# An attention-style block with three-pass fp32 matmuls: inputs centred before their split, and running maxima turned on VectorE

## The reference

```python
xn  = (x - mean_g) / sqrt(var_g + 1e-5)      # group norm, 32 groups of 8 channels, over all 4096 positions
q, k, v = split(xn @ W_qkv)                  # each 4096 x 256
k   = softmax(k over the 4096 positions)     # per channel
ctx = k^T v                                  # 256 x 256
out = x + (q ctx) @ W_out + b_out
```

## Time and profile before

| | |
|---|---|
| median of 3 runs | 1215.09 us (1214.95 to 1216.85) |
| the profiled execution | 1214.93 us, its span 1213.2 us |
| PE busy | 1190.1 us, 98% |
| DVE busy | 842.1 us, 69% |
| ACT busy | 840.1 us, 69% |
| POOL busy | 622.4 us, 51% |
| chain that ended last | PE 93%, DVE 2%, ACT 1%, POOL 1% |

### The profile page before, as it was taken

One profiled execution on the slowest core, in us unless ns is written; L12 is line 12 of the kernel. 1 busy time (PEld: TensorE's weight loads), 2 busy tenths in 40 slices (PEclk: granted clock), 3 DMA queues, 4 the chain that ended last, 5 costly groups with the idle time before them and its releaser, 6 DMA issues.

```text
span 1213.2 us, 21447 instructions
## 1 busy us (share of the span) xinstructions
PE 1190.1 (98%) x8460; PEld 1115.8 (92%) x8460; DVE 842.1 (69%) x1582; ACT 840.1 (69%) x1140; POOL 622.4 (51%) x288
## 2 busy tenths in 40 slices
PE   4999999999999999999999999999999999999998
PEld 4998999999899998999989999899999989999897
DVE  6877667676776767768776677766767676676551
ACT  5767768677685776757677686776857768577664
POOL 8664564635645355563655636356463564536520
PEclk9999999999999999999999999999999999999999
DMA  9448666576765758666486665867657576573524
GB/s 339 146 167 294 218 235 205 195 269 208 274 203 199 264 172 294 226 206 237 162 301 229 221 227 183 286 209 252 204 201 263 193 278 225 201 252 122 191 74 170
DMA packets 107077, 266.71 MB, mean 220 GB/s; under 512 B 10208, under 2 KB 10208, under 8 KB 106976
## 3 DMA queue, kind: packets, MB, share of 16 engines
q1 hardware_dynamic: 106976, 265.33, 63.5%
HBM read 198.18 MB, written 67.11 MB: 219 GB/s over the span
## 4 chain that ended last, share of the span: by engine, by line
PE 93%; DVE 2%; ACT 1%; POOL 1%; DMA 1%; issue 1%; SPq 0%; DVEq 0%; POOLq 0%; ACTq 0%
PE ps_k L399 29%; PE ps_e L564 19%; PE ps_e L573 10%; PE ps_g L492 5%; PE ps_e L480 5%; PE ps_e L492 5%; PE ps_e L482 5%; PE ps_g L480 4%; PE ps_g L482 4%; PE ps_g L511 1%; PE ps_g L528 1%; PE ps_g L542 1%; PE ps_g L534 1%; POOL x_lo L347 1%; DVE mx L892 1%
## 5 line engine op out<-in xcount | busy, mean ns | idle before, releaser
L341 POOL TENSOR_TENSOR xt_lo<-xt_raw,xt_hi 128x1024 fp32r<-128x1024 f32 x128 | 307.4, 2404 | 434.5 <-ACT xt_hi L676 309.1
L347 POOL TENSOR_TENSOR x_lo<-x_raw,x_hi 128x1024 fp32r<-128x1024 f32 x128 | 281.4, 2216 | 65.6 <-ACT x_hi L681 56.2
L892 DVE TENSOR_TENSOR mx<-ps_k,mx 128x256 f32<-128x256 f32 x480 | 203.3, 424 | 95.8 <-ACT e_raw L685 74.3
L733 ACT ACTIVATE o_stage<-ps_e,bias 128x512 f32<-128x512 f32 x253 | 170.9, 689 | 114.1 <-PE ps_e L573 114.1
L399 PE MATMUL ps_k<-wk_hi,xt_hi 128*128 128x256 f32 x1024 | 207.1, 284 | 1.0 <-DVE mx L892 0.7
L399 PE MATMUL ps_k<-wk_lo,xt_hi 128*128 128x256 f32 x1024 | 205.5, 283 | 0.0
L685 ACT ACTIVATE e_raw<-ps_k 128x512 f32<-128x512 f32 x256 | 141.4, 596 | 87.2 <-PE ps_k L399 87.2
L849 DVE BATCH_NORM_STATS2 bn<-xs 128x6 f32<-128x512 f32 x240 | 154.5, 686 | 40.7 <-DMA xs<-in_xt_dram 39.5
L693 ACT ACTIVATE e_hi<-e_raw 128x1024 fp32r<-128x1024 f32 x128 | 135.1, 1055 | 60.9 <-DVE e_raw L917 33.0
L399 PEld LDWEIGHTS ps_k<-wk_hi,xt_hi 128*128 128x128 f32 x1024 | 163.4, 190 | 8.7 <-issue 1.8
L399 PE MATMUL ps_k<-wk_hi,xt_lo 128*128 128x256 f32 x1024 | 158.2, 283 | 0.0
(11 more groups left out here) (129 smaller groups left out, 1992.7 us busy)
## 6 DMA issues: line engine op xcount, KB each, us to landing
xt_raw<-in_xt_dram SPq DMA_DIRECT2D x128, 512.0 KB, 4.3
x_raw<-in_xn_dram SPq DMA_DIRECT2D x128, 512.0 KB, 3.5
out_dram<-o_stage SPq DMA_DIRECT2D x127, 512.0 KB, 4.5
xs<-in_xt_dram SPq DMA_DIRECT2D x240, 256.0 KB, 5.1
w_setup<-in_w_dram SPq DMA_DIRECT2D x2, 256.0 KB, 10.1
out_dram<-o_stage SPq DMA_DIRECT2D x2, 256.0 KB, 2.0
wk<-in_w_dram SPq DMA_DIRECT2D x1, 256.0 KB, 9.9
wq_t<-in_w_dram SPq DMA_DIRECT2D x1, 256.0 KB, 10.9
```

The source lines that it names most:

```text
L341: nc.gpsimd.tensor_tensor(xt_lo[:, s], xt_raw[:, s], xt_hi[:, s].bitcast(F32), ALU.subtract).then_inc(xt_lo_ready, 1)
L347: nc.gpsimd.tensor_tensor(x_lo[:, s], x_raw[:, s], x_hi[:, s, :, 0:C].bitcast(F32), ALU.subtract).then_inc(x_lo_ready, 1)
L733: nc.scalar.activation(o_stage[:, u % O_SLOTS, h, :], src, ACT.Identity, bias=bias[:, h:h + 1]).then_inc(o_ready, 1)
L892: nc.vector.tensor_tensor(mx[:], tile, mx[:], ALU.max).then_inc(max_done, 1)
```

## The change

1. For images behind the first, ScalarE takes the high part of `xt` plus minus the mean (two instructions of 128 x 512 for one of 128 x 1024), and GpSimd adds minus the mean to `xt_raw` in place (`xt_centre`, two instructions of 128 x 512) before `xt_low`. The output then needs no product of the matrix with the mean: the bias is `b_out` plus the mean. `bias_sum` is left for image 0 alone.
2. `turn_max` is gone. VectorE transposes the running maximum in squares of 32 x 32, reduces each over 32, copies the results of the other three groups of 32 partitions to the first, and reduces again, so that the maxima stand as 32 x 8. It splits them into high and low part and multiplies them with two stacked 32 x 32 identities (`block_diag`); TensorE spreads them with one fp32r matmul by ones (`spread_max`). The scales between blocks are made in the 32 x 8 form and copied to 128 partitions by four copies (`spread_scales`).
3. The sums of statistics are split into high and low part as well, and `stats_mean` and `stats_var` are one fp32r matmul with 4 columns each.
4. The order: on ScalarE `xt_high(n, 0)` and `(n, 1)` come behind `x_high(b, 4)`, on GpSimd `xt_low(n, 0)` behind `x_low(b, 4)`; on TensorE both `emit_high` of the first output chunk come before its `emit_low`.

The core of the diff (left out: declarations, the first image's set-up, the splits of the statistics on VectorE, which are two casts and two subtractions of 128 x 2 per image and three more small additions):

```diff
@@ tensors @@
+        grp_r = sb("grp_r", [P, P], F32R)
+        one_r = sb("one_r", [P, 1], F32R)
+        diag = u_hi[0:2 * Q, 1, :]
+        quad = sb("quad", [P, NQ, QUADS])
+        m_blk = sb("m_blk", [Q, 2, NQ])
+        m_parts = sb("m_parts", [2 * Q, NQ], F32R)
-        bias = sb("bias", [P, CB])
+        bias = sb("bias", [P, 2, CB])
...
@@ GpSimd @@
+            def xt_centre(b, parity, j):
+                pool.wait_ge(xt_hi_ready, b * NCH + (j + 1))
+                s = slot(j, parity)
+                for c in range(CB):
+                    last = nc.gpsimd.tensor_scalar(xt_raw[:, s, c], xt_raw[:, s, c], neg_mean[:, parity, c:c + 1], None,
+                                                   ALU.add)
+                last.then_inc(xt_centred, 1)
...
+                elif more:
+                    x_low(b, 4)
+                    xt_centre(n, np_, 0)
+                    xt_low(n, np_, 0)
+                    rstd_of(n, np_)
+                    x_low(b, 5)
+                    xt_centre(n, np_, 1)
+                    x_low(b, 6)
+                    xt_centre(n, np_, 2)
+                    x_low(b, 7)
...
                     for j in range(3, NCH):
+                        xt_centre(n, np_, j)
                         xt_low(n, np_, j)
@@ TensorE @@
-            def turn_max(b, blk):
-                to = max_psum(b, blk)
-                pe.wait_ge(max_done, b * (TILES * NCH) + TILES * HALF * (blk + 1))
-                for d in range(CB):
-                    last = nc.tensor.transpose(to[:, 0, d * P:(d + 1) * P], mx[:, d * P:(d + 1) * P], ident)
-                last.then_inc(t_ps, 1)
             def spread_max(b, blk):
-                pe.wait_ge(m_blk_ready, b * 2 + (blk + 1))
-                for d in range(CB):
-                    last = nc.tensor.matmul(to[:, 1, d * P:(d + 1) * P],
-                                            m_blk[:, blk, d:d + 1].broadcast_to([P, P]), ident,
-                                            start=(d == 0), stop=True, skip_group_check=True)
-                last.then_inc(bc_ps, 1)
+                pe.wait_ge(diag_ready, b * 2 + (blk + 1))
+                nc.tensor.matmul(max_psum(b, blk)[:, 1, 0:C], one_r[0:2 * Q].broadcast_to([2 * Q, P]), diag,
+                                 start=True, stop=True).then_inc(bc_ps, 1)
             def stats_mean(b):
...
+                    pe.wait_ge(max_done, b * (TILES * NCH))
+                    pe.wait_ge(mean_parts_ready, b)
+                    nc.tensor.matmul(stats_psum(b, 0), grp_r[:], mean_parts[:].rearrange("p k c -> p (k c)"), start=True,
+                                     stop=True).then_inc(mean_ps, 1)
...
                 emit_high(b, parity, 0, 0)
-                bias_sum(b, parity)
+                if b == 0:
+                    bias_sum()
+                emit_high(b, parity, 0, 1)
                 emit_low(b, parity, 0, 0)
-                emit_high(b, parity, 0, 1)
                 emit_low(b, parity, 0, 1)
@@ ScalarE @@
             def xt_high(b, parity, j):
...
+                if j == 0:
+                    act.wait_ge(mean_read, b + 1)
+                for c in range(CB):
+                    last = nc.scalar.activation(xt_hi[:, s, c], xt_raw[:, s, c], ACT.Identity,
+                                                bias=neg_mean[:, parity, c:c + 1])
+                last.then_inc(xt_hi_ready, 1)
...
-                if more:
+                exps(b, 3)
+                x_high(b, 4)
+                if more and b:
                     xt_high(n, np_, 0)
-                exps(b, 3)
-                if more:
+                scales(b)
+                if more and b:
                     xt_high(n, np_, 1)
-                x_high(b, 4)
-                scales(b)
                 exps(b, 4)
-                if more:
+                if more and b:
                     xt_high(n, np_, 2)
                 for j in range(5, NCH):
                     x_high(b, j)
                     exps(b, j)
+                    if b == 0:
+                        xt_high(n, np_, j - 5)
@@ VectorE @@
             def block_max(b, blk):
-                src = max_psum(b, blk)
-                dve.wait_ge(t_ps, b * 2 + (blk + 1))
-                nc.vector.tensor_reduce(m_blk[:, blk, :], src[:, 0, 0:C].rearrange("p (d n) -> p d n", d=CB),
-                                        AX_X, ALU.max).then_inc(m_blk_ready, 1)
+                n = b * 2 + blk + 1
+                dve.wait_ge(max_done, n * (TILES * HALF))
+                nc.vector.transpose(turned[:], mx[:]).then_inc(turned_ready, 1)
+                dve.wait_ge(turned_ready, n)
+                nc.vector.tensor_reduce(quad[:, :, 0], turned[:].rearrange("p (q k) -> p q k", k=Q), AX_X,
+                                        ALU.max).then_inc(quad_ready, 1)
+                dve.wait_ge(quad_ready, n)
+                for r in range(1, QUADS):
+                    last = nc.vector.tensor_copy(quad[0:Q, :, r], quad[r * Q:(r + 1) * Q, :, 0])
+                last.then_inc(quad_moved, 1)
+                dve.wait_ge(quad_moved, n)
+                nc.vector.tensor_reduce(m_blk[:, blk, :], quad[0:Q], AX_X, ALU.max).then_inc(m_blk_ready, 1)
+            def block_diag(b, blk):
+                n = b * 2 + blk + 1
+                dve.wait_ge(m_blk_ready, n)
+                nc.vector.tensor_copy(m_parts[0:Q, :], m_blk[:, blk, :]).then_inc(m_part_hi_ready, 1)
+                dve.wait_ge(m_part_hi_ready, n)
+                nc.vector.tensor_tensor(m_parts[Q:2 * Q, :], m_blk[:, blk, :], m_parts[0:Q, :].bitcast(F32),
+                                        ALU.subtract).then_inc(m_part_lo_ready, 1)
...
+                dve.wait_ge(m_part_lo_ready, n)
+                nc.vector.tensor_tensor(diag.rearrange("p (q k) -> p q k", k=Q),
+                                        eye2[:].unsqueeze(1).broadcast_to([2 * Q, NQ, Q]),
+                                        m_parts[:].bitcast(F32).unsqueeze(2).broadcast_to([2 * Q, NQ, Q]),
+                                        ALU.mult).then_inc(diag_ready, 1)
+            def spread_scales(b):
+                dve.wait_ge(alpha_q_ready, b + 1)
+                by_quad = alpha_q[:].rearrange("p k (d r) -> p k d r", r=QUADS)
+                for r in range(QUADS):
+                    last = nc.vector.tensor_copy(alpha[r * Q:(r + 1) * Q, :, :], by_quad[:, :, :, r])
+                last.then_inc(alpha_ready, 1)
...
-            def bias_of(b):
-                dve.wait_ge(bias_ps, b + 1)
-                dve.wait_ge(b_mean_ready, b + 1)
-                if not (isinstance(b, int) and b == 0):
-                    dve.wait_ge(o_ready, b * (CB * NCH))
-                nc.vector.tensor_tensor(bias[:], ps_g0[:, 0, 0:CB], b_mean[:], ALU.add).then_inc(bias_ready, 1)
```

More of the change, by code:

```diff
@@ L93, in build @@
         eye = [zero_eye[:, P:3 * P], zero_eye[:, 0:2 * P]]
-        grp = sb("grp", [P, P])
+        with nc.sbuf_tensor("grp", [P, P], F32) as grp:
+            pass
+        grp_r = sb("grp_r", [P, P], F32R)
+        one_r = sb("one_r", [P, 1], F32R)
+        var_sum = sb("var_sum", [P, CB])
+        var_parts = sb("var_parts", [P, 2, CB], F32R)
+        mean_parts = sb("mean_parts", [P, 2, CB], F32R)
+        mean_rest = sb("mean_rest", [P, CB])
         mx = sb("mx", [P, C])
@@ L107, in build @@
         u_lo = sb("u_lo", [P, CB, C], F32R)
+        with nc.sbuf_tensor("turned", [P, C], F32) as turned:
+            pass
         u_hi = sb("u_hi", [P, CB, C], F32R)
+        diag = u_hi[0:2 * Q, 1, :]
         m_lo = u_lo
@@ L213, in stats_psum @@
         def stats_psum(b, which):
-            return ps_k[:, 0, 0, C + which * CB:C + (which + 1) * CB] if b == 1 else ps_k[:, 1, which, 0:CB]
+            if b == 1:
+                return ps_k[:, 0, 0, C + 2 * CB * which:C + 2 * CB * (which + 1)]
+            return ps_k[:, 1, which, 0:CB if b == 0 else 2 * CB]
         def max_psum(b, blk):
@@ L359, in _ @@
             for j in range(5):
-                xt_low(0, 0, j, first=True)
+                xt_low(0, 0, j)
             rstd_of(0, 0)
@@ new lines, in stats_var @@
+            def stats_var(b):
+                if b == 0:
+                    pe.wait_ge(var2_ready, 1)
+                    nc.tensor.matmul(stats_psum(b, 1), grp_r[:].bitcast(F32), var2[:], start=True,
+                                     stop=True).then_inc(var_ps, 1)
+                else:
+                    pe.wait_ge(var_parts_ready, b)
+                    nc.tensor.matmul(stats_psum(b, 1), grp_r[:], var_parts[:].rearrange("p k c -> p (k c)"), start=True,
+                                     stop=True).then_inc(var_ps, 1)
@@ L542, in bias_sum @@
                         last = nc.tensor.matmul(ps_g0[:, 0, h:h + 1], m_full[:, c, h * P:(h + 1) * P],
-                                                neg_mean[:, parity, c:c + 1], start=(h == 0 and c == 0),
+                                                neg_mean[:, 0, c:c + 1], start=(h == 0 and c == 0),
```

(7 more changed lines are left out.)

149 lines of the change are left out of this document (112 added, 37 removed).

## The result

The changed kernel takes 1482.53 us, the median of 4 runs (1481.58 to 1484.71), against 1215.97 us (1214.95 to 1217.3) of the kernel before beside it: a ratio of 1.219, with a 95% interval of 1.217 to 1.222. It is 22% slower. The forecast was 1271 us with a range from 1228 to 1335, so the sign was right and the size wrong by a factor of nearly five.

The account below looks back on a forecast made before the run. TensorE, busy 98%, was taken to bound the kernel. From 1214.93 us, gather waits 42, chunk 3 and 4 waits 32 and VectorE's chain 15, less 33 saved, gave +56: 1271 us, range 1228 to 1335.

Parts of the forecast that it names:

- the sign: Whole kernel: the change makes it slower, given a chance of 0.86.
- the gather's sum: Gathers 5 to 7: GpSimd's queued work ends at 295.2, TensorE is ready at 292.2 and waits 3.0 us, 14 times.
- d: GpSimd: length of one centring instruction of 128 x 512, taken as 0.7 us.
- chunk 3: Emission: two centring instructions before its low part, slack 0.40 us; TensorE waits 2d + 0.1 - 0.4 = 1.1 us.
- the third: GpSimd: centring runs at the two-input rate, d = 1.2, giving 1343 us; chance 0.09.
- the prediction's formula: Whole kernel: gathers 14 x 3.0, chunks 3 and 4 15 x 2.1, chain 15, less saving 33: +56 us.
- the other three: GpSimd's tight hand-overs: low parts of xt chunks 3 and 4 and x chunk 7, slack 0.40, 0.68 and 0.93 us.
- ScalarE's pair: Two activations of 512 in place of one of 1024 for xt's high part: ends 0.1 us later.
- Covered: Gather: ScalarE runs 2.1 us later with xt 0 and 1 moved, but GpSimd's queue runs later still, so no cost.
- The chain of VectorE: Block 0's maxima on VectorE: last two-SBUF-input instructions wait for GpSimd, 1.0 us per image, 15 us in all.
- Rival 2: Block 0: VectorE's copies take the lock too, the chain ends 3.5 us late, 1308 us; chance 0.18.
- The saving: TensorE: removed bias, turning and spreading products, 2.65 us less 0.44 for replacements: 2.2 us per image, 33 us.

## Why the prediction was wrong

**Right.** The sign; that GpSimd's slack was what counted; and the form of the gather's sum. The prediction has GpSimd busy there for 11.8 + 6d. With d = 1.56 that is 21.2, and the rows above give 21.23. For chunk 3, 2d - 0.4 plus what ScalarE's pair takes longer (below) is 3.0, measured 2.91. Of the rivals the third, d = 1.2, is nearest in mechanism and, at 1343, in time.

**The step that failed: the length of the centring, d.** I took 0.7 because the fill was nearest, and the upper bound was half of a two-input instruction of 1024, 1.20. That was no bound. It rests on the belief that one input costs at most what two do, and the runs show the reverse: 1.56 for 512 columns with one input and a scalar from memory, 1.90 for 1024 with two. The Trainium skill's 1.03 cycles per element for short loop bodies (GPSIMD Engine Reference, Elementwise — side-by-side cycle accounting), by which I had estimated near 0.55, is farther off; this trace has 3.05 ns per column of a row (1.56 us / 512). (The time that I gave for it, about 1246, was also mis-added: my own sum at 0.55 gives 1249.) With d = 1.56 the prediction's formula gives 14 x 8.2 + 15 x 5.6 + 15 - 33 = +181 for the +56 forecast. So d is 125 of the 212 us that were missing.

**Places left out.** Chunks 5 to 7 of the emission, 2.45 us per image, 34 us. Measured in the trace of before as the other three were, GpSimd's slack is 1.5 us for chunk 6 and 2.2 for chunk 7 (means of images 2 to 13): no less than two centring instructions by my d (1.4), far under them by the real one (3.1). Chunk 5 is not waited for, its low part is ready 1.3 us early even after the change; its 0.72 us are products at half rate behind the wait for chunk 4. I had looked for tight places with a price in mind, and stopped where the price was met. Half of the centring moves nine tenths of its length to the end, which no sum over three places can give.

**Image 0.** 27 us, where I had about one. Its chain of maxima waits for GpSimd's low parts of e and of an x chunk (the copies at 53.43 take 4.68 us), TensorE 6.5 us for it, and the centring of the next image's first chunks stands behind x chunk 7, so that the first keys wait 1.8 and 4.1 us.

**ScalarE's pair** takes 1.33 us in place of 1.05, so 0.28 and not 0.1, and its two high parts in front of x 5 to 7 cost what the kernel without centring shows, 1.8 us per image, where they are not under the centring. "Covered" held only because the centring was longer.

**The chain of VectorE.** Taken at 1.0 us per image; in the full change it is nothing but for image 0, and alone it is 69 us. Rival 2 had the mechanism, copies that take the lock. My argument against it (tiny, back to back) failed: GpSimd's instruction does come in between, and each copy or cast can lose a whole one. It was covered by the larger stall.

**The saving** was counted 2.2 us per image. The places show about 1.5: the bias product gives 0.92 as said (0.89), the two turns 0.6, but the spreading on 64 rows takes 0.31 and slows its neighbour by 0.09, for the 0.12 assumed, so it saves nearly nothing. On 128 rows it takes the 0.12.

**The clock.** Not in the prediction at all. Chunk 4's list says 1.39 where the formula, with ScalarE's longer pair, has 2.9: the missing 1.5 us are the ten products from 577.06 to 580.94 at half rate. The end set by GpSimd is the same. A list of waits therefore understates such a stall; the distance from start to start does not.

What stays open: some 33 us, 2.4 per image, by which the foreseen places (9.74 + 6.37) exceed the formula with the measured d (8.2 + 5.6). The half-rate stretches, ScalarE's longer pair and its new order lie there, and were not told apart.

## What to carry to other kernels

A bottleneck engine that never waits says nothing of the slack of those that feed it. Before work goes to an idle engine, take the slack of every hand-over in the period, not of the tightest, and price the new instruction by a row of the same kind (inputs, scalar, columns); where there is none, the nearest rows of another kind are not bounds. Two costs that wait in the same stretch do not add, so a part that looks harmless inside a change may be worth most of its gain or loss alone.

On VectorE beside a busy GpSimd, write small moves within SBUF as reductions, and keep one input of a two-input instruction in PSUM: here that gave 58 and 15 us, where nothing larger covered them.
